# A second scan module spread over layer 2's attention: two groups in every head

## The reference, cut to what matters

```python
# layer 2 attention: 16 heads of 128, 4 batches
q = rmsnorm(x @ Wq); k = rmsnorm(ctx @ Wk); v = ctx @ Wv
x = x + tanh(g) * softmax(q k^T / sqrt(128)) v @ Wo
# layer 2 feed-forward: 8 experts of 176 (top 2) and a shared expert of 352
x = x + tanh(g) * (sum_e w_e * Wd_e(silu(Wg_e x) * Wu_e x) + shared(x))
# layer 3 attention: state-space scan over 256 steps, 256 channels, 16 states
state = state * exp(delta * A) + delta * u * B ;  y = sum_n state * C
x = x + tanh(g) * (y + D * u) * silu(layernorm(x))
# layer 3 feed-forward: 32 + 16 experts, top 4
```

## Time and profile before

| | |
|---|---|
| profiled execution | 1301.26 us, span 1299.5 us |
| attention of layer 2 | about 507 to 837 us of the span |
| feed-forward of layer 2 | 850 to 1020 us |
| a full head of the attention | 20.54 us |
| busy over the span | TensorE 83%, VectorE 66%, GpSimd 55%, ScalarE 51% |

### The profile page before, as it was taken

How to read it: one execution, slowest core, us unless ns; L and a number is a source line. 1 busy time by engine, 2 the same in 40 slices (tenths; PEclk the granted TensorE clock), 3 DMA queues, 4 the chain that set the end, 5 groups by cost and what they waited for, 6 DMA issues and landing times.

```text
span 1299.5 us, 18166 instructions
## 1 busy us (share of the span) xinstructions
PE 1081.3 (83%) x5382; PEld 839.8 (65%) x5383; DVE 863.2 (66%) x1521; ACT 666.3 (51%) x1702; POOL 713.6 (55%) x480
## 2 busy tenths in 40 slices
PE   6486587778748888999999999799999737999992
PEld 3465576667515665888888888665555536887781
DVE  3886999888778975666666566769987772322221
ACT  4475355445472215777787777467652134333330
POOL 1107888888723223445444554439975205888873
PEclk8887899899868988999999999889989758999996
DMA  6594899896540004011101110304543993555566
GB/s 186 163 169 131 215 279 291 231 259 147 76 126 0 1 3 123 29 55 51 54 18 54 56 45 1 102 6 146 150 137 84 275 224 67 84 83 82 81 79 133
DMA packets 141110, 146.06 MB, mean 112 GB/s; under 512 B 34181, under 2 KB 127357, under 8 KB 141029
## 3 DMA queue, kind: packets, MB, share of 16 engines
q1 hardware_dynamic: 115556, 110.71, 29.3%
q0 software_dynamic: 24384, 33.31, 15.9%
q10 hardware_dynamic: 1088, 1.05, 0.3%
HBM read 119.04 MB, written 25.99 MB: 112 GB/s over the span
## 4 chain that ended last, share of the span: by engine, by line
PE 46%; POOL 16%; DVE 13%; issue 13%; DMA 6%; ACT 4%; another core or an unknown queue 0%; SPq 0%; ACTq 0%; POOLq 0%; DVEq 0%
PE bank L1629 4%; PE bank L1725 4%; PE bank L1692 4%; PE bank L1714 4%; PE bank L2497 3%; POOL f_sums L1050 3%; PE bank L2159 3%; DMA f_sums<-arena,put 3%; POOL arena L1036 3%; POOL y L2407 2%; PE bank L1618 2%; PE bank L1647 2%; PE bank L1703 2%; POOL arena L586 2%; DMA e_sums<-ctxT,put 2%
## 5 line engine op out<-in xcount | busy, mean ns | idle before, releaser
L566 DVE TENSOR_TENSOR_SCAN arena<-arena 128x1024 f32<-128x1024 f32 x64 | 154.3, 2411 | 14.4 <-issue 10.7
L1050 POOL DMA_INDIRECT f_sums<-arena,put x64 | 126.1, 1971 | 27.1 <-issue 15.6
L586 POOL TENSOR_TENSOR arena<-arena 128x1024 f32<-128x1024 f32 x32 | 82.4, 2575 | 94.4 <-DVE arena L566 94.4
L1036 POOL DMA_INDIRECT arena<-y_rows,slots x64 | 84.8, 1324 | 65.4 <-DVEq L1253 46.2
L2398 POOL DMA_INDIRECT e_sums<-ctxT,put x63 | 100.0, 1587 | 25.4 <-issue 16.2
L2497 PE MATMUL bank<-arena,ssm_y 128*128 x504 | 109.9, 362 | 3.2 <-ACT ssm_y L2566 1.4
L544 ACT ACTIVATE arena<-arena,ssm_A 128x255 f32<-128x255 f32 x256 | 107.9, 499 | 2.0 <-DVE arena L488 1.8
L2159 PE MATMUL bank<-yT,arena 128*128 128x512 f32 (+1 forms) x224 | 105.5, 616 | 2.2 <-ACT arena L2090 2.2
L596 PE MATMUL bank<-arena,ident 128*128 128x256 f32 x256 | 69.5, 419 | 36.3 <-DVE arena L586 32.8
L2679 DVE TENSOR_SCALAR ctxT<-bank,slot_w 128x256 f32<-128x256 f32 x63 | 30.5, 484 | 97.1 <-DMA e_sums<-ctxT,put 79.0
L555 DVE TENSOR_TENSOR arena<-arena 128x1024 f32<-128x1024 f32 x64 | 93.8, 1466 | 0.8 <-DMA arena<-bc_rows 0.7
(11 more groups left out here) (343 smaller groups left out, 2778.7 us busy)
## 6 DMA issues: line engine op xcount, KB each, us to landing
arena<-bc_rows SPq DMA_DIRECT2D x64, 512.0 KB
arena<-in_L_ffn_w_gate_dram SPq DMA_DIRECT2D x16, 256.0 KB
arena<-in_L_ffn_w_up_dram SPq DMA_DIRECT2D x16, 256.0 KB
arena<-in_L_ffn_w_down_dram SPq DMA_DIRECT2D x16, 256.0 KB
x<-in_L_ffn_w_gate_dram SPq DMA_DIRECT2D x16, 256.0 KB
y<-in_L_ffn_w_up_dram SPq DMA_DIRECT2D x16, 256.0 KB
yT<-in_L_ffn_w_down_dram SPq DMA_DIRECT2D x16, 256.0 KB
arena<-in_L_ffn_Wd_dram SPq DMA_DIRECT2D x1, 3072.0 KB, 18.0
```

The source lines that it names most:

```text
L566: nc.vector.tensor_tensor_scan(ssm_h[:, j % 2, :], ssm_decay[:, j % 2, :], ssm_in, 0.0, ALU.mult, ALU.add).then_inc(s_ssm_h, 1)
L586: ops.tensor_tensor(ssm_hC_buf[:, j % 2, :], ssm_h[:, j % 2, :], ssm_C[:, g % 2, :], ALU.mult).then_inc(s_ssm_hC, 1)
L1036: nc.gpsimd.indirect_dma_start(out=f0_xg[:, n % RING, e, :], out_offset=None, in_=y_rows, in_offset=bass.IndirectOffsetOnAxis(ap=slots[:, ...
L1050: nc.gpsimd.indirect_dma_start(out=f0_sums[m % SUMS], out_offset=bass.IndirectOffsetOnAxis(ap=put[:, m:m + 1], axis=0), in_=f0_ye[:, n % R ...
```

## The change

The attention takes 31 of the 32 groups. Group 2h (`x_main(h)`) keeps the place that group h had in head h. Group 2h-1 (`x_extra(h)`), from head 1 on, has its decay on ScalarE at the end of step 3 of head h-1, its product on VectorE in step 0 of head h, its scan in step 1, and its C product and sums on GpSimd ahead of those of group 2h. The loads for the next head's pair are issued by SyncE once in every head, after the weights of the head (before: once in two heads, ahead of them); in head 0 the pair's loads now come before that head's weight loads. The sums of batches 0 to 2 are added in step 0 of heads 5, 9 and 13. Group 31 alone remains in the feed-forward, in step 1, so `g_last` goes from 22 to 1. The step of `e_early_sp` becomes max(3, g_last + 1), which is 3; it still waits for all of `s_ssm_red_y`, whose last count is in VectorE's step 3.

```diff
-        def x_group(h):
-            return divmod(h, GB * HC)
+        XG = GROUPS - 1
+        def x_main(h):
+            return divmod(2 * h, GB * HC)
+        def x_extra(h):
+            return divmod(2 * h - 1, GB * HC)
...
             for h in range(H):
-                if h and h % HC == 0:
-                    b, j = x_group(h)
-                    ssm_load_sp(sp, 1, b, j // HC)
-                head(h // HB, h % HB)
                 if h == 0:
                     ssm_load_sp(sp, 1, 0, 0)
+                head(h // HB, h % HB)
+                if h + 1 < H:
+                    b, j = x_main(h + 1)
+                    ssm_load_sp(sp, 1, b, j // HC)
...
                 if b == 1:
-                    ssm_act(act, 1, *x_group(i * HB + k))
+                    ssm_act(act, 1, *x_main(i * HB + k))
+                if b == 3 and not beyond(i * HB + k + 1):
+                    ssm_act(act, 1, *x_extra(i * HB + k + 1))
...
                 if b == 2:
-                    ssm_in_product(dve, 1, *x_group(h))
+                    ssm_in_product(dve, 1, *x_main(h))
                 elif b == 3:
-                    ssm_scan(dve, 1, *x_group(h))
+                    ssm_scan(dve, 1, *x_main(h))
+                elif h:
+                    (ssm_in_product, ssm_scan)[b](dve, 1, *x_extra(h))
...
-                if b == 1 and h and x_group(h)[1] == 0:
-                    ssm_out_dve(dve, 1, x_group(h)[0] - 1)
+                if b == 0 and h >= 2 and x_extra(h - 1)[1] == GB * HC - 1:
+                    ssm_out_dve(dve, 1, x_extra(h - 1)[0])
...
-                ssm_out_pool(pool, 1, *x_group(h))
+                if h:
+                    ssm_out_pool(pool, 1, *x_extra(h))
+                ssm_out_pool(pool, 1, *x_main(h))
...
-        XG = H
...
-                if t == g_last + 1:
+                if t == max(SH, g_last + 1):
                     e_early_sp(sp)
...
-            ssm_out_dve(dve, 1, g_group(XG)[0] - 1)
```

## The result

The changed kernel took 1318.3 us (median of 4 runs, 1315.1 to 1321.4) against 1300.5 for the kernel before: 1.0147, with a 95% interval of 1.0115 to 1.0180. The forecast was 4 us faster, the range ended at 1315.

The account below looks back on a forecast made before the run. It took TensorE to bound the attention and the scan on VectorE and GpSimd the feed-forward. 1301.26 - 24 + 12 + 8 = 1297.3 us profiled, 1296.5 us as median (0.7 us lower); range 1282 to 1315.

Parts of the forecast that it names:

- What bounds the kernel: TensorE bounds the attention; in the feed-forward the scan on VectorE and GpSimd is the bound.
- What the groups free in the feed-forward: Fifteen groups leaving the feed-forward take off 24.0 us: 20.0 from block 6's turn on, 4.0 ahead; bounds 20 and 24.
- The early loads: Feed-forward: moved to step 3, they hold up block 6 on SyncE's queue, 12 us back; bounds 0 and 20.
- The decay on ScalarE: Attention, step 3: a second decay makes the probabilities' copy late, 0.2 us x 14 heads = 3 us; bounds 0 and 6.
- The second product and scan in ordinary heads: Attention, VectorE steps 0 and 1: nearly fit the slack, 0.1 us x 13 = 1.5 us.
- the rival: Attention: GpSimd's C product takes the port before VectorE's scan, some 22 us in place of 1.5: 1317; chance 0.23.
- The batch adds: Attention, step 0 of heads 5, 9, 13: three adds wait for GpSimd's sums, 0.3 us each, 1 us.
- The last head: Attention's last head has short steps; the extra product and scan make it 2.5 us late; bounds 1 and 4.

Follow-up runs that it names:

- e1_late: The changed kernel with the six early expert loads back in step 23 of the feed-forward: 1305.9 us, 1.0082 of the kernel before.
- e2_rows: The changed kernel with GpSimd summing every group straight into ssm_y and no VectorE batch adds: 1305.0 us, 1.0042 of the kernel before.
- e7_nudge: e3_late_rows with two tiny memsets on VectorE right before the scan of step 3: 1293.7 us, 0.9961 of the kernel before.
- e3_late_rows: The changed kernel with the edits of both e1_late and e2_rows: 1287.5 us, 0.9927 of the kernel before.
- e4_late_rows_last: e3_late_rows with only one group in the last head, so groups 30 and 31 remain in the feed-forward: 1282.7 us, 0.9889 of the kernel before.
- e11_nudge_order: e7_nudge with GpSimd made to wait for the scan of step 3 before the extra group's C product: 1289.3 us, 0.9929 of the kernel before.

## Why the prediction was wrong

**What bounds the kernel:** right. The feed-forward without its fifteen groups runs without a gap; e1_late shows it.

**What the groups free in the feed-forward: the term that failed first.** Forecast 24.0 us; e1_late has 14.3. I had counted 26 steps where there are 28: 14 column blocks in two halves. The page before the change had the row for it, and the count is the same after:

```profile
L2159 PE MATMUL bank<-yT,arena 128*128 128x512 f32 (+1 forms) x224 | 105.5, 616 | 2.2 <-ACT arena L2090 2.2
```

224 matmuls at 8 to a step are 28. The stretch behind the turn of block 6 is thus two steps longer, 2 x 5.17 = 10.3 us: 100.3 bare in place of 90.0, and 9.7 gained in place of 20.0. With the 4.0 ahead of it 13.7, against 14.3 measured. The price per step, taken from undisturbed rows, was right to half a us over the stretch; the count has to be read as well.

**The early loads:** right in mechanism and nearly in size: 12 us forecast, of which 9 of waiting and 3 of clock; 10.5 and 2.6 in the trace, 13.2 by e1_late. The landing order of the earlier trace rows was enough for it. The block was held up earlier than I had it, though: it was not issued and then queued behind the loads, SyncE could not issue it before 926.29. In the trace after, SyncE was held in the issue of the six loads for 30 us; before it was 26 (997.9 to 1024.3).

The Trainium skill, DMA: Bandwidth & Descriptors, section Queues, rings and completion order, has descriptors consumed in ring order on each DMA engine. The trace after agrees as far as it goes: the 3072 KB landed 23.2 us after their issue, the 2048 KB, issued 0.5 us later, after 28.3.

**The decay on ScalarE:** forecast 3 us, measured nothing: the heads of e2_rows are 20.5 with it. TensorE's weight load waits 0.54 us for the copy, but the matmul that uses it starts as early in the head as before (716.25, that is 4.86 us behind the same matmul of the step before; 4.86 before the change too).

```profile
716.12 0.75 PEld L1713 LDWEIGHTS bank<-arena 128*128 128x128 f32 x4 [0.54 <-ACT arena L1830]
```

**The second product and scan in ordinary heads:** forecast 1.5 us, by which the scan of step 3 wins the port. In the changed kernel GpSimd won it in six heads, 4.4 us in all (0.86 + 0.66 + 0.66, twice). The point from which the rival decides, a margin of 0.3 us, was given; both sides of it were met. In e7_nudge the rival is true in ten heads, but at 0.7 us a head, 6.9 us, not 22: the scan is 1.9 us longer there and TensorE waits 0.39, while the price had been put at nearly the whole delay.

**The batch adds: the step that failed in the attention.** Forecast 1 us, as a wait for GpSimd's sums. What the runs show in its place: the two adds read both inputs from SBUF, meet GpSimd's product of the next group, and take 3.2 us for 0.8. That is 6.4 us in the three heads (2.1, 2.1, 2.3; the lost port in the first two is left out), and two of the heads behind run at a lower clock, 5.1 us more. The trace before had the row for it: in the feed-forward such a pair took 3.37 us under GpSimd's work.

```profile
933.74 3.37 DVE L626 TENSOR_TENSOR ssm_y<-ssm_y,arena 128x256 f32<-128x256 f32 x2
```

I had priced the product and the scan by the port, but not the adds.

**The last head:** 2.5 us forecast, 5.3 measured with the norms behind it (50.2 for 44.9), 3.4 without batch adds (e3_late_rows against e4_late_rows_last). Right in kind, too small.

**Sum:** -24 + 12 + 8 = -4 forecast. By the runs: -14.3 + 13.2 in the feed-forward and in the attention 6.4 + 5.1 + 4.4 + 5.3, less 1.2 in its first head (22.2 for 23.4) and 0.5 ahead of it: 19.5. With the rest and the start +19.2, as the two spans have it. Of the 23 us between forecast and profile 9.7 are what the groups free (10.3 for the two steps, less 0.6 that came ahead of them), 10.5 the batch adds and their clock, 2.9 the port, 2.8 the last head and 2 the loads and the rest. Against them stand 3 for the decay, which cost nothing, and the 1.7 of the first head, which are luck: no term foresaw them.

## What to carry to other kernels

Where GpSimd and VectorE both work from SBUF, plan by who comes first: put the one with slack behind the other by a semaphore (and look at where it has none: in the short last head of e11_nudge_order that wait cost 3 us), and price every two-input instruction of VectorE with the longest GpSimd instruction that may stand beside it, the small ones above all. When the last user of a buffer moves forward, look at what that releases: a bulk load that was harmless at the end of a stage stood here ahead of the weights that the stage lived on. And count the steps of a stage from the page's instruction counts before multiplying.

## What the runs showed of the hardware that I had not expected

- A lead of 0.02 us (585.49 against 585.51) was enough for VectorE's scan to hold off GpSimd's product, and 0.30 us the other way made the scan 4.2 us. Two memsets, which put the scan off by 0.02 us, turned one into the other and cost 6.9 us in ten heads.
- TensorE's clock after a wait of 1.8 us: in the changed kernel the first batch add was followed by a head of 20.5 us, the second by one of 22.6 at a granted clock of 0.92, the third by 23.6 at 0.87. The same wait had a price of 0, 2 or 3 us, and which one could not be told from the wait.
- The first head of the same attention took 23.4, 22.2 or 20.5 us from run to run, at a granted clock of 0.88, 0.92 or 1.00, whichever kernel it was. Compared by whole stages, two single profiles differ by up to 3.4 us for this alone.
